# A vision block with sixteen experts on one core: the input norm's root first, expert counting split around the attention rows, the early table behind them, rows ahead of the first weights

## What is computed

```python
def reference(x, ...):
    h = tok(x)                                   # patches, three levels, fused to 192 channels
    h = h + attn(layernorm(h))
    h = h + ffn(layernorm(h))
    return h

def attn(x):
    q, k, v = split(x @ w_qkv)                   # 12 heads of 16
    a = softmax(q @ k.T / 4)
    y = (a @ v) @ w_out + b_out
    return (y - mean(y)) * rsqrt(var(y) + eps) * ln_g + ln_b

def ffn(x):
    probs = softmax(x @ Wr.T)
    top_p, top_idx = top_k(probs, 2)             # two of 16 experts for each token
    y = 0
    for e in range(16):
        y += gate_e * (gelu(x @ W1[e] + b1[e], exact) @ W2[e] + b2[e])
    return x + y
```

## Time and profile before

| | us |
|---|---|
| median of 3 runs | 800.95 |
| lowest, highest | 797.98, 802.77 |
| the profiled execution | 795.69 |
| its span (first to last instruction) | 794.0 |

### The profile page before, as it was taken

The page is one execution under the profiler, slowest core; times in us unless marked ns, Lnnn a source line. Parts: engine busy times, 40 slices in busy tenths (PEclk is TensorE's granted clock), DMA queues, the critical chain, the costliest instruction groups (busy, mean ns, idle before and its releaser), DMA issues.

```text
span 794.0 us, 22662 instructions
## 1 busy us (share of the span) xinstructions
PE 698.3 (88%) x7845; PEld 602.2 (76%) x7845; DVE 454.2 (57%) x1318; ACT 367.1 (46%) x882; POOL 387.6 (49%) x599
## 2 busy tenths in 40 slices
PE   3207879999999999999988989999999999999995
PEld 3106756677777777777666878999999999998995
DVE  7102035678888888888877736434444445443448
ACT  1002225666666666666656333434443354433352
POOL 7760022356777777777757544333333333332422
PEclk9999999999999999999989999999999999999998
DMA  8629255434444444444415933566725741669659
GB/s 186 158 50 197 46 109 120 103 99 110 109 117 111 107 112 110 111 108 112 114 47 145 273 95 100 163 168 177 208 67 149 208 119 55 183 156 261 184 190 342
DMA packets 96715, 110.68 MB, mean 139 GB/s; under 512 B 18418, under 2 KB 84979, under 8 KB 96307
## 3 DMA queue, kind: packets, MB, share of 16 engines
q1 hardware_dynamic: 79122, 79.56, 39.0%
q0 software_dynamic: 11792, 27.18, 11.6%
q10 hardware_dynamic: 5712, 2.79, 2.1%
HBM read 142.13 MB, written 33.96 MB: 222 GB/s over the span
## 4 chain that ended last, share of the span: by engine, by line
issue 36%; PE 17%; POOL 16%; DVE 13%; another core or an unknown queue 6%; POOLq 4%; DMA 3%; SPq 3%; ACT 2%; DVEq 0%; ACTq 0%
POOL pixels L761 5%; PE BK L877 4%; POOL slot_rows L1951 3%; PE BK L1011 3%; POOLq L760 3%; DVE negmax L1622 2%; POOL pair_rows L751 2%; PE BK L970 2%; POOL rs L1900 2%; PE BK L990 2%; POOL hr L1940 2%; PE BK L931 1%; PE BK L1022 1%; DVE hr L745 1%
## 5 line engine op out<-in xcount | busy, mean ns | idle before, releaser
L539 ACT ACTIVATE pixels<-BK,shared 128x128 f32<-128x128 f32 x474 | 131.1, 375 | 194.3 <-PE BK L496 147.1
L496 PE MATMUL BK<-pixels,shared 64*128 64x128 f32 x2844 | 174.9, 273 | 3.5 <-issue 2.6
L496 PEld LDWEIGHTS BK<-pixels,shared 64*128 64x128 f32 x2844 | 169.5, 188 | 6.9 <-issue 5.5
L751 POOL DMA_INDIRECT pair_rows<-pixels x79 | 78.3, 992 | 197.1 <-DVE pixels L714 172.5
L515 PE MATMUL BK<-shared,pixels 64*128 64x192 f32 x1752 | 160.3, 328 | 2.5 <-DVE pixels L714 1.3
L515 PEld LDWEIGHTS BK<-shared,pixels 64*128 64x128 f32 x1752 | 142.4, 187 | 4.4 <-issue 4.3
L1622 DVE TENSOR_REDUCE negmax<-BK 128x6 f32<-128x1536 f32 x64 | 112.4, 1757 | 25.7 <-PE BK L990 23.2
L1368 ACT ACTIVATE shared<-BK 128x1536 f32<-128x1536 f32 x64 | 92.8, 1449 | 10.2 <-PE BK L1011 9.0
L1951 POOL DMA_INDIRECT slot_rows<-xr,adr x64 | 64.9, 1014 | 36.7 <-issue 14.6
L700 DVE TENSOR_TENSOR pixels<-pixels 128x1 int32<-128x1 f32 x60 | 9.6, 160 | 106.6 <-PE BK L482 106.6
L990 PE MATMUL BK<-shared 96*128 96x256 bf16 x384 | 53.9, 277 | 3.8 <-DVE negmax L1622 2.3
(11 more groups left out here) (245 smaller groups left out, 1164.4 us busy)
## 6 DMA issues: line engine op xcount, KB each, us to landing
shared<-ew SPq DMA_DIRECT2D x150, 288.0 KB
shared<-ew SPq DMA_DIRECT2D x75, 576.0 KB
shared<-qk_parts SPq DMA_DIRECT2D x112, 96.0 KB
shared<-expert_biases SPq DMA_DIRECT2D x75, 99.0 KB
pixels<-slot_rows POOLq DMA_DIRECT2D x64, 104.0 KB
qk_parts<-shared SPq DMA_DIRECT2D x32, 192.0 KB, 2.0
shared<-qk_parts SPq DMA_DIRECT2D x16, 288.0 KB
shared<-pair_rows SPq DMA_DIRECT2D x12, 384.0 KB, 4.2
```

The costliest lines, as they stand in the source:

```text
L496: last = nc.tensor.matmul(hidden(t)[h * HC + c], w1h[w][rows, (k + h) % NK, c * P:(c + 1) * P], xtT[p][rows, k, :], start=(c == 0 and k == ...
L539: last = nc.scalar.activation(hT[p][:, c * P:(c + 1) * P], hidden(t)[c], ACT.Gelu, bias=bias[w][:, c:c + 1])
L751: nc.gpsimd.indirect_dma_start(pair_d, bass.IndirectOffsetOnAxis(t_dst[:, t:t + 1], 0), ysum[t % NB][:, :], None).then_inc(s[f"m_sc{t % NB ...
```

## The change

Four places, one for each part of the title.

1. GpSimd, in every step: the root of the input norm (rs1, image i + 2) is taken ahead of the root of the attention's norm (rs2, image i - 2).
2. VectorE, in every step: `b_count` is cut in two. `b_hot` (the zeros and ones and their sum) stays between `b_on(.,0)` and `b_on(.,1)`; the two additions to the running counts go behind `b_on(.,1)`. In the drain too for image 12; for images 13 to 15 both halves stand together where `b_count` stood.
3. VectorE, early table: `early_tiles` (the shift to tiles and the first two additions) goes between a_max(14,2) and a_max(14,3); `early_ends` keeps its place with the last two additions. In the drain `early_lists`, now with the reduction to `r_tfs`, goes behind `b_on(14,0)`.
4. SyncE: the rows of tiles 0 and 1 are issued ahead of the weights of tile 0.

The hunks below are of GpSimd's step, VectorE's counting, VectorE's step (two places), VectorE's drain and SyncE's loads, in this order.

```diff
             def step(i, p, on):
...
                 if on(-3):
                     res(i - 3)
+                if on(2):
+                    rsqrt(rs1, mv1, var1, s["dve_mv1"], s["dve_x1"], s["pool_var1"], s["pool_rs1"], i + 2)
                 if on(-2):
                     rsqrt(rs2, mv2, var2, s["dve_mv2"], s["dve_yn"], s["pool_var2"], s["pool_rs2"], i - 2)
-                if on(2):
-                    rsqrt(rs1, mv1, var1, s["dve_mv1"], s["dve_x1"], s["pool_var1"], s["pool_rs1"], i + 2)
...
-            def b_count(j, p):
+            def b_hot(j):
                 dve.wait_ge(s["dve_pick"], 5 * j + 2)
                 for k in range(TOPK):
...
                 nc.vector.tensor_tensor(cnt[:, :, :], hot[:, 0, :, :], hot[:, 1, :, :], ALU.add).then_inc(s["dve_pick"], 1)
+
+            def b_count(j, p):
                 dve.wait_ge(s["dve_pick"], 5 * j + 4)
                 nc.vector.tensor_tensor(cum[:, p, 1, :], cum[:, p, 0, :], cnt[:, 0, :], ALU.add).then_inc(s["dve_pick"], 1)
...
                 if on(2):
                     f_hst(i + 2)
+                if isinstance(i, int) and i == SEEN + 3:
+                    early_tiles(dve)
                 if on(0):
                     a_max(i, 3)
...
                 if on(-1):
                     b_on(i - 1, 0)
                 if on(-3):
-                    b_count(i - 3, q)
+                    b_hot(i - 3)
                 if on(-1):
                     b_on(i - 1, 1)
+                if on(-3):
+                    b_count(i - 3, q)
...
                 early_entries(dve)
+                b_on(k, 0)
                 early_lists(dve)
-                b_on(k, 0)
+                b_on(k, 1)
+                b_hot(m)
                 b_count(m, m % 2)
-                b_on(k, 1)
...
+            rows(0)
+            rows(1)
             one = chosen(0)
             first(0, *one)
-            rows(0)
-            rows(1)
             two = chosen(1)
```

26 lines of the change are left out of this document (17 added, 9 removed).

## The result

The changed kernel takes a median of 791.02 us (789.13 to 793.18, 4 runs) beside 800.10 us (797.98 to 802.77, 4 runs) for the kernel before on the same chip. The ratio is 0.9886, with a 95% interval of [0.984, 0.9931]: 9 us faster, between 5.5 and 12.8. Run again later in more rounds (24 runs of the kernel before, 12 of the changed one) it came to 0.993 [0.9908, 0.9952], between 3.8 and 7.3 us and 5.6 in the middle. The first pair has only four runs of each, and its median for the kernel before, 800.10, lies 4 to 7 us above every later one (793.31 to 795.91), so the later ratio is the better measure of the gain. Predicted were 794.0 us and a gain of 7.0.

What follows compares the result with a forecast made beforehand. TensorE was taken as the bound in loop and expert tiles. 5.3 (loop) + 2.3 (step 14) - 0.6 (lists) = 7.0 us, so 788.7 for the profiled execution and 800.95 - 7.0 = 794 as median; range 789.5 to 800.5.

Steps and rivals of the forecast that it cites:

- if tiles from 500 us start less than 6 us earlier: Expert tiles: one of three signs that would show the prediction wrong.
- The loop: Attention steps 4 to 13: swapped roots and split counting gain 5.3 us, bounds 3.4 and 7.3.
- the two ties: Loop, VectorE with TensorE: two chains of 18.80 and 20.11 us, together 38.91 for two images, 19.46 for one.
- 20.02 now: Loop: time of one image before the change, against which 19.46 gave 0.56 an image, 5.6 over ten.
- TensorE's recorded idle, which is all that can go: Loop: 3.4 + 1.2 + 5 x 0.14 = 5.3 us of waits, taken as the gain.
- My upper bound: Loop: 7.3 us, 0.73 an image, if overlaps at the joints also close; chance 0.10, then 792.
- The rival that f_x1 is held: Loop, VectorE: f_x1 stands still beside rs2's root; only the counting's 3.3 stays, sum 5.0, 796 us; chance 0.10.
- b_hot caught twice: Loop, VectorE: b_hot's last addition also waits for GpSimd's L1932; 0.83 us more an image, at worst 802.2; chance 0.07.
- Step 14: Early table on VectorE: moved additions shorten TensorE's idle and the clock stays up; gain 2.3 us, bounds 0 and 2.8.
- The lists: Drain: early_lists behind b_on(14,0) makes the lists later by b_on's length; cost 0.6 us, bounds 0 and 1.1.
- The first tiles: Rows issued ahead of tile 0's weights: change 0 us, bounds 0.3 gain and 1 loss.
- Whatever TensorE gains by having them early it loses again in the wait before 439.29: First tiles: early rows 0 gain nothing, as TensorE waits for tile 3's rows before 439.29 anyway.

Runs made afterwards that it cites:

- e8_after: The changed kernel run again without an edit; ratio 0.993 [0.9908, 0.9952] to the kernel before.
- e11_qk_first: The changed kernel with b_count's two additions one place later, behind f_qk(.,0); 787.34 us, ratio 0.9904 [0.9871, 0.9937] to the kernel before.
- e6_norows: The changed kernel with the old order of the first loads, tile 0's weights ahead of the rows; ratio 0.9941 [0.9919, 0.9963] to the kernel before.
- e7_lists: The changed kernel with early_lists ahead of b_on(14,0) again in the drain; ratio 0.9908 [0.988, 0.9936] to the kernel before.

## Why the prediction was right, and where it was not

**The total.** 788.7 was worked out for the profiled execution, and it came to 789.13. That agreement is luck in good part: the loss of 2.5 us behind the lists was met by 2.4 us at the start and the end, which scatter by more than that, and the second profiled execution of the same kernel took 795.49, as long as the one of before (795.69). What stands is the timed gain, 5.6 us with 3.8 to 7.3 as its interval, beside 7.0.

One of my own signs of being wrong did come: "if tiles from 500 us start less than 6 us earlier". The product of tile 15 starts at 506.00 us where it started at 511.24, 5.2 earlier, and at 511.64 in e8_after. The lists do come 7.7 us earlier (7.0 was said), so what is missing was lost behind them. As the start alone moves by up to 5 us between executions, a sign in absolute times was a poor one.

**The loop: mechanism right, size 0.6 us too large.** 5.3 us were forecast over ten steps, 4.7 came. Every sign named is there: f_x1 without idle, the input norm's root first, no wait ahead of either transposes, two images in 39.0 where 38.91 was worked out. Of the two ties, the one from a_max(.,0) to the `on` transposes was put at 18.80 and takes 319.84 - 301.12 = 18.72. The one from the `on` transposes over GpSimd's queue to the next a_max(.,0) was put at 20.11 and takes 320.61 - 300.37 = 20.24. It holds the held addition and f_qk, and these now set the pace, as e11_qk_first shows by taking the additions out of it. What I missed is that this tie has a wait on TensorE in it, ahead of the key projection (0.24 us in step 9, 0.31 in step 10): its first part, 5.16 in the prediction, takes 305.77 - 300.37 = 5.40. The ties thus gave 19.46 an image, and 19.49 came.

The two steps that were off stand elsewhere in the working. The first is the image of before, "20.02 now": it was read from one pair, and the ten steps took 199.57, so 19.96 each; by that the ties would have given 5.0. The second is "TensorE's recorded idle, which is all that can go", from which the 5.3 was taken. The waits fell from 5.3 (4.6 recorded) to 3.0 and the loop still gained 4.7, so overlaps at the joints, which no wait shows, came back as well, and a new wait took some of the room. The prediction reckoned 0.14 us for the unrecorded wait ahead of `on`, and that joint was worth 0.30. My upper bound, with the joints closed, was the right idea with no allowance for the new wait.

**Which part does it.** The prediction gave the swap of the roots 3.4 of the 5.3 us, by the waits' total in the earlier trace rows, and the counting 1.2 and the rest. The runs give the swap 1.5 over ten images alone and 0.6 beside the split counting, and the counting 4.0 alone. A wait's length measures what its engine loses there, not what returns when it is taken away. The rival's own working had this: without the roots, 3.3 were left for the counting (it measured 4.0). Of the parts' timed runs only those of the counting alone (0.9923 [0.9884, 0.9961]) and both together (0.9953 [0.9926, 0.998]) stand clear of no change.

**The rival that f_x1 is held** did not come. In the changed kernel ten of the instructions that make xn start beside rs2's root with 0.46 us of it left, and take 0.369 to 0.370 us. All 32 together:

```profile
L1600 DVE TENSOR_SCALAR xn<-hr,mv,rs x32: 369/372/395, 92.5 to 372.0; 128x192 f32 x20, 128x192 f32<-128x192 f32 x12
```

The Trainium skill (SBUF — State Buffer, section Who interferes with whom) says that tensor_scalar can enter a mode with two ports, when its operands meet certain conditions, and is then shut out for the whole of a GpSimd instruction. As the rival took that rule, the trace disagrees: a held one would have taken at least 0.46 us, and these take 0.37. The same section says that an instruction with two SBUF inputs contends with a GpSimd instruction that reads SBUF. By that rule, the trace agrees: the sum of 32 columns, L1700, takes 0.93 us under L1947 in the step shown.

The root beside f_x1 isn't always undisturbed, though. In the ten loops with the swap it takes 0.69 to 0.71 us in 95 of 100 images, and 0.81 or 0.82 in five: once in e6_norows and four times in e7_lists (the row below, step 10). In the 40 images of the four loops without the swap it is always 0.69. Each of the four makes its image in e7_lists some 0.17 us longer, and that is most of why this loop takes 195.8 us where the others with the same code take 194.9 or 195.0. All five start 95 to 107 ns behind the start of f_x1, and all that start at most 92 ns behind it take 0.69 to 0.71 us. So it is a matter of some ns between the two engines; why it is so, is open.

```profile
314.96 0.82 POOL L1918 TENSOR_TENSOR rs<-var,mhalf 128x2 f32<-128x2 f32 x1
```

**b_hot caught twice** did not come. b_hot is caught once in each step of the loop, as it was before. There the row that was held changed from image to image: the comparisons (1.09 us for the two, step 9) or the sum (0.87, step 10). Now it is always the sum, 925 ns at the median, and the additions behind b_on(.,1) no longer hold up the transposes. The cost of this rival has a wrong term besides: its 4.34 from a_max(.,0) to L1906 is 309.64 - 304.94 = 4.70 in the rows of before, and 4.65 after.

**Step 14: right, against an execution with a window.** 2.2 measured beside 2.3. The order of events was the forecast one: the additions in idle time, a wait of 0.77 (0.7 was said), no window. The idle time was put at 1.1 us and is worth 0.4 to 0.7 where the clock stays up anyway; the rest is there only when the clock would have fallen, as it did in the execution of before that I compared with.

**The lists: right, and hidden by the clock.** b_on(14,0) costs 0.6, e7_lists against the changed kernel. The window of before reached 2.7 us past a_max(15,0) and cost 0.5 in the same stretch, and with it gone this came back. I had counted the window's cost up to a_max(15,0) only.

**The first tiles: the clock left out.** I took 0 with a loss of 1 at most, and the two traces of the changed kernel lost 2.5 and 5.2 us between the lists and tile 15. The step at fault is "Whatever TensorE gains by having them early it loses again in the wait before 439.29". The issue of tile 3's rows moved just as said (13.81 for 13.89), TensorE came to tile 0 1.5 us sooner behind the lists, and its pauses grew to 1.31 and 1.78 us, 3.1 together, for 1.5 before. So the gain was lost again, as said, but I priced the pauses by their length and not by the clock that can fall behind them, though in step 14 I had priced the clock. That the order of the loads brings this loss isn't shown. e11_qk_first, with the same drain and the same order, takes 89.3 us from the lists to tile 15, 0.6 less than before, and the timed runs of e6_norows and e8_after don't differ. In how many executions the clock falls there is open, and so is why tile 3 to tile 15 varies from 61.3 to 65.4 us.

## What to carry to other kernels

When two waits follow each other in one loop, price them by the row that ends last after the edit, engine by engine, and not by their totals: 3.4 us of recorded waits were worth 1.5 at most, and 1.2 were worth 4.0. A short operation with two SBUF inputs on VectorE lasted here until the GpSimd row that it fell under was over (0.93 us for 0.19), so give it a place behind which nobody waits; moving it once more, behind f_qk, gave another 2.8 us. Before a microsecond from a trace is put down to an edit, profile the same kernel twice: two such traces differed by 2.7 us behind the lists, and a loop with the same code by 0.9.
